# Splitting the block-mask preparation in two halves, with four reduction tiles and two output staging tiles, in an eight-core transformer layer kernel

## The reference

```
bm  = mask.reshape(Nb, 32, Kb, 32).sum(axis=(1, 3)) > 0      # 128 x 128 blocks of 32 x 32
w   = weight * bm (each block of 32 x 32 kept or zeroed)
x   = layernorm(x + x @ w.T + bias)                          # eps 1e-5, no scale, no shift
p   = top2(softmax(x @ Wr.T)), renormalized                  # 8 experts
h   = x @ A[e].T                                             # rank 16 for each expert
ffn = x @ Wb.T + bias2 + 2 * sum_e p[e] * h[e] @ Bm[e].T
x   = layernorm(x + ffn)
```

## Time and profile before

| | us |
|---|---|
| two runs of the kernel | 3265.05 and 3376.0 (median 3320.53) |
| the profiled execution | 3265.14 |
| its span, slowest core (5) | 3263.6 |
| spans of the eight cores | 3234.6 to 3263.6 |
| PE busy | 2417.1 (74%) |
| DVE busy | 892.8 (27%) |
| ACT busy | 405.5 (12%) |

### The profile page before, as it was taken

The page is one execution under the profiler, slowest core; times in us unless marked ns, Lnnn a source line. Parts: engine busy times, 40 slices in busy tenths (PEclk is TensorE's granted clock), DMA queues, the critical chain, the costliest instruction groups (busy, mean ns, idle before and its releaser), DMA issues.

```text
span 3263.6 us, 49199 instructions; the slowest of 8 cores (3234.6 to 3263.6 us)
## 1 busy us (share of the span) xinstructions
PE 2417.1 (74%) x21109; PEld 1949.3 (60%) x21109; DVE 892.8 (27%) x1573; ACT 405.5 (12%) x417; POOL 90.6 (3%) x158
## 2 busy tenths in 40 slices
PE   1457575757573888888629999659999469968994
PEld 1345454535452667677528888538888358856883
DVE  1553535353433111111122222222222122222221
ACT  0001111111112221212220000110000210010002
POOL 2000000000000000000000000000000000000000
PEclk9677777778685999999869999769999789978997
DMA  9856565655430465664672333203333655522543
GB/s 95 149 116 135 104 131 104 131 111 125 92 92 1 106 132 131 122 141 107 159 204 81 93 95 104 57 1 82 106 81 107 158 156 140 153 82 70 144 134 130
DMA packets 264256, 364.00 MB, mean 112 GB/s; under 512 B 38626, under 2 KB 173794, under 8 KB 249570
## 3 DMA queue, kind: packets, MB, share of 16 engines
q0 software_dynamic: 50224, 119.63, 22.9%
q1 hardware_dynamic: 204602, 207.66, 22.6%
q10 hardware_dynamic: 9216, 33.56, 2.7%
HBM read 377.69 MB, written 102.76 MB: 147 GB/s over the span
## 4 chain that ended last, share of the span: by engine, by line
PE 69%; ACT 9%; DVE 9%; DMA 6%; issue 5%; ACTq 1%; POOL 0%; DVEq 0%; SPq 0%; POOLq 0%
PE pmm L463 58%; ACT wtb L430 6%; DVE bs2t L339 4%; PE pmm L458 3%; DMA out<-outstg 3%; DVE wstg L396 2%; PE pT L577 2%; PE pT L417 2%; ACT xnat L679 2%; ACT outstg L662 1%; DMA xnat<-xin 1%; PE pH L819 1%; DMA mstg<-mask 1%; PE pmm L472 1%; DMA wstg<-w 1%
## 5 line engine op out<-in xcount | busy, mean ns | idle before, releaser
L463 PE MATMUL pmm<-wtb,x1t 128*128 128x256 bf16 x16384 | 1925.5, 277 | 0.0
L463 PEld LDWEIGHTS pmm<-wtb,x1t 128*128 128x128 bf16 x16384 | 1584.8, 99 | 261.3 <-issue 2.8
L483 DVE SCALAR_TENSOR_TENSOR xnat<-pmm,xnat 128x256 bf16<-128x256 f32 x512 | 217.5, 425 | 1800.2 <-PE pmm L472 924.7
L430 ACT ACTIVATE wtb<-pT 128x1024 bf16<-128x1024 bf16 x256 | 247.8, 1021 | 1221.8 <-PE pT L417 1220.9
L577 PE MATMUL pT<-ident,xnat 128*128 128x128 bf16 x1024 | 107.6, 284 | 267.6 <-ACT xnat L679 101.7
L417 PE MATMUL pT<-ident,wstg 128*128 128x128 bf16 x2048 | 190.3, 256 | 147.4 <-DVE wstg L396 82.2
L417 PEld LDWEIGHTS pT<-ident,wstg 128*128 128x128 bf16 x2048 | 154.9, 115 | 181.8 <-issue 176.1
L577 PEld LDWEIGHTS pT<-ident,xnat 128*128 128x128 bf16 x1024 | 90.7, 130 | 284.3 <-issue 280.7
L487 DVE BATCH_NORM_STATS2 bnbt<-xnat 128x6 f32<-128x256 bf16 x512 | 218.6, 427 | 52.8
L458 PE MATMUL pmm<-wtb,ones 1*128 1x256 bf16 x512 | 142.9, 279 | 53.1 <-ACT wtb L430 51.0
L630 ACT ACTIVATE stdt<-vpe 128x1 f32<-128x1 f32 x32 | 6.5, 203 | 1412.8 <-DVE vpe L623 1405.1
(11 more groups left out here) (54 smaller groups left out, 327.3 us busy)
## 6 DMA issues: line engine op xcount, KB each, us to landing
wts<-wtb SPq DMA_DIRECT2D x32, 2112.0 KB, 16.5
mstg<-mask POOLq DMA_DIRECT2D x32, 1024.0 KB, 9.6
wstg<-w POOLq DMA_DIRECT2D x32, 1024.0 KB, 9.9
wstg<-wb POOLq DMA_DIRECT2D x32, 1024.0 KB, 10.4
out<-outstg ACTq DMA_DIRECT2D x64, 512.0 KB, 7.6
xnat<-xin POOLq DMA_DIRECT2D x16, 1024.0 KB, 11.9
wstg<-am POOLq DMA_DIRECT2D x1, 1024.0 KB, 10.4
wstg<-bm POOLq DMA_DIRECT2D x8, 128.0 KB, 13.7
```

Of the source, the lines that this page charges most:

```text
L430: sC.inc(sc.activation(wtb[slw][:, :].rearrange("p (kt n) -> p kt n", n=NCW) [:, gp * 8:(gp + 1) * 8, sub * 128:sub * 128 + 128], pT[kk][: ...
L463: mm = t.matmul(pmm[bk][:, 0:NCW], x1t[:, kt * maxchunk + i * 128: kt * maxchunk + (i + 1) * 128], wtb[sl][:, kt * NCW:(kt + 1) * NCW], st ...
L483: sV.inc(v.scalar_tensor_tensor(sl_ap, pmm[bk][:, 0:NCW], 1.0, sl_ap, ALU.mult, ALU.add))
```

## The change

maskpipe is cut in two. maskpipe_a holds the load of the mask tile and the reduction to bs2t; maskpipe_b holds the two small matmuls, bm4t and q2full. There are four bs2t tiles instead of two, each freed by the matmul that reads it. Ahead of pass 0 stand the first halves of tiles 0 to 5 and the second halves of tiles 0 to 3, interleaved; at the end of pass nci stand the first halves of tiles 2 nci + 6 and 2 nci + 7, then the second halves of 2 nci + 4 and 2 nci + 5. Of the output staging tiles outstg there are two instead of three. The weights, the matmuls and every shape are the same.

```diff
@@ -126,12 +126,11 @@
         wrt = sbuf("wrt", [128, KT * E], BF16)
         wstg = [sbuf("wstg0", [128, D], BF16), sbuf("wstg1", [128, D], BF16)]
         mstg = [sbuf("mstg0", [128, D], BF16), sbuf("mstg1", [128, D], BF16)]
-        bs2t = [sbuf("bs2t0", [128, 128], F32), sbuf("bs2t1", [128, 128], F32)]
+        bs2t = [sbuf(f"bs2t{i}", [128, 128], F32) for i in range(4)]
         bm4t = [sbuf("bm4t0", [4, 128], BF16), sbuf("bm4t1", [4, 128], BF16)]
         q2full = sbuf("q2full", [128, KT * 128], BF16)
         outstg = [sbuf("outstg0", [128, D // 4], F32),
-                  sbuf("outstg1", [128, D // 4], F32),
-                  sbuf("outstg2", [128, D // 4], F32)]
+                  sbuf("outstg1", [128, D // 4], F32)]
         g_t = sbuf("g_t", [128, maxchunk], BF16)
         wselt = sbuf("wselt", [E, maxchunk], BF16)
         wsele = sbuf("wsele", [128, maxchunk], BF16)
@@ -318,9 +317,12 @@
 
 
         q2_ready = [0] * KT
-
-        def maskpipe(ntt):
+        red_ready = [0] * KT
+        bs2_free = [None] * 4
+
+        def maskpipe_a(ntt):
             sl = ntt % 2
+            s4 = ntt % 4
             gres = [None]
 
             @block.gpsimd
@@ -332,25 +334,30 @@
             gs, gv = gres[0]
 
             @block.vector
-            def _(v, ntt=ntt, sl=sl, gs=gs, gv=gv):
+            def _(v, sl=sl, s4=s4, gs=gs, gv=gv, bf2=bs2_free[s4]):
                 v.wait_ge(gs.h, gv)
-                if state["maskpipe_free"][sl]:
-                    v.wait_ge(sV.h, state["maskpipe_free"][sl])
+                if bf2 is not None:
+                    v.wait_ge(bf2[0].h, bf2[1])
                 sV.inc(v.tensor_reduce(
-                    bs2t[sl][:, :].unsqueeze(2),
+                    bs2t[s4][:, :].unsqueeze(2),
                     mstg[sl][:, :].rearrange("p (kb j) -> p kb j", j=32),
                     AX, ALU.add))
             state["mstg_free"][sl] = sV.n
-            red_v = sV.n
+            red_ready[ntt] = sV.n
+
+        def maskpipe_b(ntt):
+            sl = ntt % 2
+            s4 = ntt % 4
 
             @block.tensor
-            def _(t, sl=sl, red_v=red_v):
+            def _(t, s4=s4, red_v=red_ready[ntt]):
                 t.wait_ge(sV.h, red_v)
                 if state["pq_free"]:
                     t.wait_ge(sV.h, state["pq_free"])
                 sT.inc(t.matmul(pQ[0:4, 0:128], e4tf[:, :],
-                                bs2t[sl][:, :], start=True, stop=True))
+                                bs2t[s4][:, :], start=True, stop=True))
             tv = sT.n
+            bs2_free[s4] = (sT, sT.n)
 
             @block.vector
             def _(v, sl=sl, tv=tv):
@@ -372,7 +379,6 @@
                 sV.inc(v.tensor_copy(q2full[:, ntt * 128:(ntt + 1) * 128],
                                      pQ[:, 128:256]))
             state["pq_free"] = sV.n
-            state["maskpipe_free"][sl] = sV.n
             q2_ready[ntt] = sV.n
 
         def gen_subtile(L, ntt):
@@ -493,7 +499,13 @@
         def layer_pass(L, c, nt, lora, lora_gate=None):
             if c == 0 and L == 0:
                 for ntt in range(4):
-                    maskpipe(ntt)
+                    maskpipe_a(ntt)
+                maskpipe_b(0)
+                maskpipe_a(4)
+                maskpipe_b(1)
+                maskpipe_a(5)
+                maskpipe_b(2)
+                maskpipe_b(3)
             for nci in range(NNC):
                 sl = nci % 2
                 if c == 0:
@@ -538,9 +550,12 @@
                     state["wtb_scrw"][sl] = hres[0]
                     state["scr_done"][L] = hres[0]
                     if L == 0:
+                        for ntt in (nci * 2 + 6, nci * 2 + 7):
+                            if ntt < KT:
+                                maskpipe_a(ntt)
                         for ntt in (nci * 2 + 4, nci * 2 + 5):
                             if ntt < KT:
-                                maskpipe(ntt)
+                                maskpipe_b(ntt)
                 else:
                     fw = state["wtb_free"][sl]
                     sd = state["scr_done"][L]
@@ -644,10 +659,10 @@
 
             applies = []
             if write_out is not None:
-                ofree = state.setdefault("outstg_free", [None, None, None])
+                ofree = state.setdefault("outstg_free", [None, None])
                 for qt in range(4):
                     slo = state.setdefault("outslot", [0])
-                    k = slo[0] % 3
+                    k = slo[0] % 2
                     slo[0] += 1
                     ob = outstg[k]
                     of = ofree[k]
```

## The result

| | before | after |
|---|---|---|
| median of 41 and 42 runs, us | 3268.95 | 3273.05 |
| ratio of after to before, 95% interval | | 1.0017 [1.0009, 1.0025] |
| profiled execution's slowest span, us | 3263.6 | 3267.3 |

The change makes the kernel slower by 0.17%, some 5.5 us: a small difference, but the 95% interval does not reach 1. The medians hold some executions with a lower clock on one die, which the ratios leave out, so the ratios are what is compared. With 39 more runs the median of before is 3268.95, not the 3320.53 of the first two.

A forecast was written before the change was run, and what follows sets the result against it. The prediction took the kernel to be bound by TensorE, except where it stands still for preparation. It summed 3265.1 - 26.5 (passes) + 14 (start) + 22 (two outstg tiles) = 3274.6, say 3275 us, range 3250 to 3306.

The forecast's parts named there:

- Part 3: Hand-overs and end: two outstg tiles instead of three make ScalarE's quarters wait, +22 us, bounds +2 and +56.
- Part 1: First-layer passes: one TensorE trip and the stall between reductions go, pass 13 has no reductions; -26.5 us.
- The choice between the bounds: First-layer passes: a value between -10 and -37 us, since the second L351 still waits for pQ to be read.
- the third rival: First-layer passes: reductions slip under the matmuls, each pass saves 10 us; 3161 us in all, chance 3%.
- The shorter gap buys no clock: First matmuls after each pass's gap: a gap shorter by 1.3 us gives no higher clock, so nothing was added.
- Part 2: Start: two mask loads now stand ahead of w0 and w1 on POOL's queue, delaying the first matmuls; +14 us.
- The xin load and all behind it move by 1.8 us a period: Hand-overs: each period grows by one quarter's 1.81 us, over 11 periods 19.8 us.
- the 16.4 us named as a check: Hand-overs: predicted time between xin loads in the changed trace, against 14.6 us in the kernel before.
- the ring is free: Hand-overs: two outstg tiles cost nothing if transfers are the limit, +2 us; 3255 us in all, chance 24%.
- it catches its tail: Hand-overs: the fourth quarter is itself held until the xin load lands, +56 us; 3309 us in all, chance 13%.
- a landing of 10.4 us: Hand-overs: profile row the sum followed, a quarter behind an xin load landing only after that load.

The follow-up runs named there:

- split_ring3: The changed kernel with three outstg tiles again, the four bs2t tiles lying in the third; ratio to the kernel before 0.9944.
- pq_two: The changed kernel with sums of odd mask tiles in a second PSUM bank and both first matmuls issued ahead; ratio to the kernel before 0.9962.
- hide_red: The kernel before with maskpipe split and its mask reductions placed between the evacuations of each pass; ratio to the kernel before 0.9594.
- late45_ring3: The changed kernel with three outstg tiles, first halves of mask tiles 4 and 5 behind pass 0's first bias load; ratio to the kernel before 0.9926.
- ring2_only: The kernel before with two outstg tiles instead of three and nothing else; ratio to the kernel before 1.0061.
- ring1_only: The kernel before with a single outstg tile instead of three; one run, 3387.33 us.

## Why the prediction was right or wrong

**Outcome.** The forecast of +9.5 us on the profiled execution, a loss too small to count, has the sign of what was measured and not quite twice its size (1.0017 is 5.5 us). Two steps failed. One is a term of the sum: Part 3, the ring of two output tiles, was put at +22 us and measured +16.2, and that is more than the 4 us by which the sum was too high. The other is the reference: the text named 3275 us beside a median of 3320.53, of 3265.05 and 3376.0. Read against that median, 3275 is a gain of 1.4%, while the kernel lost 0.17%. The text said that its figures were for executions like the profiled one, and the later runs of before, with a median of 3268.95, bear that out; but a forecast of a difference this small has to be stated as a ratio to the same kind of execution.

**Part 1, the passes.** Predicted -26.5 us, -25.8 in the medians (-29.8 in split_ring3). The mechanism was right, but that the number fits so well is luck: the gaps between the passes gave 31.9 us, 5.4 more than reckoned, and 6.6 us went back into the first token tiles. From the first reduction to the first multiply the gain of 1.27 us a pass was 1.48 in the timeline (13.04 to 11.56). Over 13 passes of all cores it was 1.15, for the pass that was read is one of the longer ones (median 12.71 before, 11.56 after). Pass 13 went from first compare to multiply in 2.60 us for the 3.0 that were reckoned. The rest lies where the prediction put nothing. From the first multiply to the first bias matmul the median fell from 15.12 to 14.50 us, with the mean granted clock of that stretch up from 0.58 to 0.66 of full speed; in the first tile that follows it is down from 0.74 to 0.68. "The shorter gap buys no clock" thus holds for the sum and not for its parts. Why the clock came back earlier and was lower in the tile behind was not tried, and since the first tiles differ so much between cores, part of the 6.6 us can be their spread. The choice between the bounds, that the second trip stays because of pq_free, was tested by itself: pq_two took 16 us off the passes, 10.3 of them in the gaps, by removing that wait and the serial trip with it. The order of DVE was read rightly, against the third rival: no reduction ran during matmuls. hide_red, where they do, gained 138.5 us in the passes for the 140 which the rival's mechanism promised.

**Part 2, the start.** Predicted +14 us, with the first big matmul near 164. In the changed kernel's timeline it is 165.86, on a core whose first reduction came 1.6 us later than that of the core predicted from, so 13.9 us of growth. Measured from each core's own first reduction it is 13.0 in the median; the 16.4 of the table hold some 3 us of the spread between the cores. The wait named as the cause, for the landing of w1, is there: w1 landed at 155.4, where 153.5 was reckoned. late45_ring3 took 12.9 us away by moving the first halves of two mask tiles alone.

**Part 3, the ring.** The mechanism held: the third quarter takes the fourth's place and the fourth follows 1.81 us later, and a quarter behind an xin load lands after it. The step that failed is the period's growth, put at 1.8 us with "The xin load and all behind it move by 1.8 us a period": it was 1.5 in the median of single periods, and 1.3 for each of the 11 gates when the two hand-overs (+7.4 and +6.7 us) are shared out. The step took the xin load's landing as fixed. It lands sooner the fewer quarters stand behind it: after 11.4 us with three (before; 10.9 to 11.4 in all runs with three tiles), 10.8 and 10.7 with two (the changed kernel and ring2_only), 10.2 with one (ring1_only). And in the first hand-over the stretch behind the last xin load did not grow at all: 15.6 us before, 14.9 after. The term came to 16.2 us for 22, and to 16.4 in ring2_only. A second fault is smaller: the period of 14.6 us was that of core 5, and the median over the cores was 14.1, so the 16.4 us named as a check would have been 15.9 even with a growth of 1.8.

**The rivals.** That the ring is free would have given 3255; ring2_only excludes it. That it catches its tail would have made a period of 19 us; the quarter issued 0.46 us ahead of the xin load landed after 3.6 us, as before. (Its sum, 3265.1 - 26.5 + 14 + 56, is 3308.6.) Both were decided by the rows named for them.

The rule of the Trainium skill, DMA: Bandwidth & Descriptors (Queues, rings and completion order), by which each DMA engine takes turns between the queues that have work, packet by packet, was weighed against a landing of 10.4 us. The changed kernel's quarters behind an xin load land after 9.3 and 8.6 us in the median over the cores, and those issued when none is under way after 3.0 and 3.4, so the row was the better guide to the time. The packet records of the kept traces say where the time goes. In the hand-over from chunk 0 to 1 of the kernel before, a quarter's first packet starts 0.84 us after its issue when no xin load is under way, and 6.0 us after it (median of the eight cores) when one is. Once both queues have packets running, they run side by side, some 15 packets a us of the load (8 KB each) and 21 of the quarters (4 KB). So the trace agrees with the rule, roughly, for packets that have started; the some 5 us before the first are what makes the landing late. What holds that first packet back was not tried.

## What to carry to other kernels

A split into two halves hides work only if the first half moves ahead of something long on the same engine; here it stood behind the same evacuations, and moving it between them was worth 4%, and 5.7% with the multiplies moved too and each load issued where its tile comes free, where the split gave tenths. Look at what a prologue now queues ahead of the first critical load, and at the buffer that was given up to make room: each can cost as much as the edit gains. State a small difference as a ratio, and take it from the stages of all cores, each measured from an event of its own, rather than from two spans.

## What was not expected

Two cores ran a whole stage at a lower granted clock while the others, two of them on the same die, did not. In the profiled run of split_ring3, cores 0 and 1 took 562.9 and 562.7 us from the first to the last bias matmul of chunk 0's layer 1, and the others 524.6 to 524.9 (524.6 to 527.9 in the kernel before). The windows of cores 0 and 2 (columns as in the earlier trace rows):

```profile
1080.00:1580.00 500.00, 444.06 (x3689) 346.99 (x3688) 69.86 (x164) 108.50 (x112) 22.05 (x42) 0.85 0.55 119
```

```profile
1080.00:1580.00 500.00, 437.44 (x3977) 353.88 (x3974) 75.84 (x178) 115.90 (x120) 22.05 (x42) 0.96 0.57 128
```

The same stretch holds 3689 matmuls on core 0 and 3977 on core 2, at a mean granted clock of 0.85 against 0.96 of full speed: 38 us on one core pair, seven times the change's effect. What sets it off was not tried. The start also varies from core to core within one execution (127.1 to 152.5 us to the first bias matmul in the kernel before). Most of that spread is there already at the first reduction of the mask (86.8 to 107.2 us), ahead of everything that the versions here changed.
